# A fused convolution, linear attention and mixed feed-forward kernel: the state matmuls, the halves of z and the orders of the first phase

## The reference

```python
x = einsum('oc,bchw->bohw', inv(I - ricker_circulant(width, damp)), x)   # x: 16 x 128 x 32 x 32
t = tokens(x)                                    # 16 batches x 1024 tokens x 128
# linear attention, 8 heads of 16, on u = layernorm(t)
Q, K = elu(u @ W_q.T) + 1, elu(u @ W_k.T) + 1;  V = u @ W_v.T
S = cumsum(K outer V, over tokens);  z = cumsum(K, over tokens)
t = t + ((Q . S) / max(Q . z, 1e-6)) @ W_out.T
# feed-forward, whose weights are merged per batch by a gate, on u = layernorm(t)
g = mean over tokens(relu(u @ gfc1_w.T + gfc1_b) @ gfc2_w.T + gfc2_b)
W1m, b1m, W2m, b2m = base + g mixed with the 8 task vectors
t = t + layernorm(u + relu(u @ W1m.T + b1m) @ W2m.T + b2m) * lng + lnb
```

## Time and profile before

| | us |
|---|---|
| median of 3 runs | 847.6 (845.93 to 848.53) |
| the profiled execution | 848.7 |
| its span, first to last instruction | 846.9 |
| last start of `make_qk` (tile 128 of 128) | 547.6 |
| first instruction after the first phase's tiles on VectorE | 571.2 |

### The profile page before, as it was taken

How to read it: one execution, slowest core, us unless ns; L and a number is a source line. 1 busy time by engine, 2 the same in 40 slices (tenths; PEclk the granted TensorE clock), 3 DMA queues, 4 the chain that set the end, 5 groups by cost and what they waited for, 6 DMA issues and landing times. The chain is left out here.

```text
span 846.9 us, 37199 instructions
## 1 busy us (share of the span) xinstructions
PE 739.7 (87%) x11168; PEld 538.4 (64%) x11168; DVE 742.6 (88%) x2736; ACT 670.2 (79%) x1875; POOL 534.6 (63%) x1009
## 2 busy tenths in 40 slices
PE   1588999999999999999999999968899998899994
PEld 1255666666666666666666666648577777577773
DVE  6587999999999999999999999955788985689894
ACT  1477898999989989998898988844788885688884
POOL 5486888888888888888988988810133342033333
PEclk9888999999999999999999999977999999999998
DMA  2255444454444444544454444410022221122222
GB/s 80 52 126 118 98 111 105 92 117 109 91 111 106 105 105 100 116 106 99 106 111 95 116 100 98 88 33 26 2 77 86 77 74 51 38 64 76 74 87 75
DMA packets 165473, 74.10 MB, mean 87 GB/s; under 512 B 139212, under 2 KB 152687, under 8 KB 165368
## 3 DMA queue, kind: packets, MB, share of 16 engines
q1 hardware_dynamic: 165432, 73.58, 36.0%
HBM read 22.69 MB, written 17.30 MB: 47 GB/s over the span
## 5 line engine op out<-in xcount | busy, mean ns | idle before, releaser
L795 DVE SCALAR_TENSOR_TENSOR scores_lo<-p_a,scores_hi 128x512 f16<-128x512 f32 x256 | 164.0, 682 | 0.0
L698 ACT ACTIVATE scores_hi<-p_a 128x512 f16<-128x512 f32 x256 | 138.5, 600 | 6.4 <-PE p_a L543 6.2
L861 POOL TENSOR_TENSOR stats<-stats,consts 128x1 f32<-128x1 f32 x128 | 78.1, 610 | 75.7 <-DVE stats L745 75.6
L1312 POOL TENSOR_TENSOR ffn_rstd_shift<-ffn_rstd_shift,consts 128x4 f32<-128x4 f32 x32 | 36.7, 1146 | 132.8 <-DVE ffn_rstd_shift L1271 132.8
L886 POOL TENSOR_TENSOR qk_parts<-qk_f,qk_parts 128x128 f16<-128x128 f32 x256 | 104.9, 429 | 0.1
L867 POOL TENSOR_TENSOR stats<-stats,consts 128x1 f32<-128x1 f32 x128 | 89.0, 695 | 18.7 <-DVE stats L751 17.1
L560 PE MATMUL p_o<-v_parts,scores_hi 128*128 128x17 f16 x1024 | 90.2, 171 | 12.1 <-ACT scores_hi L698 6.2
L560 PEld LDWEIGHTS p_o<-v_parts,scores_hi 128*128 128x128 f16 x1024 | 80.4, 96 | 30.0 <-issue 27.6
L1095 PE MATMUL psb<-merged_W_of_batch,h_hi 128*128 128x128 f16 x512 | 94.2, 220 | 4.9 <-DVE h_lo L1249 3.8
L1249 DVE TENSOR_TENSOR h_lo<-h_f,h_hi 128x512 f16<-128x512 f32 x128 | 95.0, 782 | 1.2 <-ACT h_hi L1152 1.2
L1141 ACT ACTIVATE h_f<-psb,merged_b_of_batch 128x512 f32<-128x512 f32 x128 | 87.0, 711 | 11.4 <-PE psb L1076 11.3
(11 more groups left out here) (195 smaller groups left out, 3009.6 us busy)
## 6 DMA issues: line engine op xcount, KB each, us to landing
x_f<-in_x SPq DMA_DIRECT2D x32, 256.0 KB, 2.9
t_rows<-t SPq DMA_DIRECT2D x64, 128.0 KB, 1.9
t_back<-t_rows SPq DMA_DIRECT2D x32, 256.0 KB, 2.6
out<-out_tile SPq DMA_DIRECT2D x32, 256.0 KB, 2.0
tv_share<-in_L_ffn_tv_W SPq DMA_DIRECT2D x32, 128.0 KB, 2.2
qkT_parts<-qk_parts SPq DMA_TRANSPOSE x128, 3.1
base_ffn_weights<-in_L_ffn_W SPq DMA_DIRECT2D x2, 256.0 KB, 4.3
W_hi_lo_rows<-base_parts SPq DMA_DIRECT2D x4, 128.0 KB, 3.8
```

Of the source, the lines that this page charges most:

```text
L698: nc.scalar.activation(ah[:, t % 2, cols], p_a[:, cols], ACT.Relu).then_inc(ahi_ready[eo], 1)
L795: nc.vector.scalar_tensor_tensor(al[:, t % 2, cols], p_a[:, cols], 0.0, ah[:, t % 2, cols], ALU.max, ALU.subtract).then_inc(alo_ready[eo], 1)
```

## The change

Five things are done, all of them in the first phase; the code of the second is the same.

- **State.** `state` makes each head's block alone: 16 matmuls with 64 columns of weights and 17 or 16 columns of output, even heads into partitions 0 to 63 and odd ones into 64 to 127. The off-diagonal blocks are never written (the bank is cleared once), so the mask multiplication is gone. `state_hi` is a ScalarE copy out of PSUM, `state_lo` a VectorE subtraction out of PSUM; GpSimd has no part in it.
- **z.** `z_hi` (ScalarE) and `z_lo` (GpSimd) split z in SBUF, before it is turned, and SyncE turns both parts with one transposing DMA of 128x256 float16. TensorE's `turn_z` and VectorE's `z_lo` are gone. `gate` waits for that DMA.
- **High parts.** `q_hi` moves from ScalarE to GpSimd.
- **Banks.** `gate` moves from p_m1 to p_m2, beside `turn_out`.
- **Orders.** All five tables are new. The last skew grows from 8 to 11, so two batches are written out ahead of the loop and two behind it.

```diff
-TENSOR_ORDER = [("conv", 0), ("project", 0), ("turn_out", 5), ("gate", 8), ("values", 4), ("turn_z", 7),
-                ("state", 2), ("out_project", 5), ("scores", 2)]
+TENSOR_ORDER = [("scores", 3), ("conv", 0), ("gate", 11), ("state", 2), ("project", 0), ("out_project", 6),
+                ("values", 4), ("turn_out", 5)]
...
+GPSIMD_ORDER = [("split_x", 0), ("rsqrt2", 9), ("z_lo", 10), ("q_hi", 1), ("k_hi", 1), ("rsqrt1", 0), ("qk_lo", 1)]
+SYNC_ORDER = [("turn_z", 10), ("load_x", 3), ("load_tv", 3), ("store", 8), ("turn", 1)]
...
-        zh = sb(top, "zT_hi", [P, NT * P], F16)
-        zl = sb(top, "zT_lo", [P, NT * P], F16)
+        zz = sb(top, "zT_hi_lo", [P, 2, NT * P], F16)
+        zh, zl = zz[:, 0, :], zz[:, 1, :]
...
             def run(eng, order, stages):
                 stages = [(skew, stages[name]) for name, skew in order]
-                batch(stages, 0, old=False)
-                with eng.Fori(1, B) as b:
+                for b in range(2):
                     batch(stages, b)
-                batch(stages, B, new=False)
+                with eng.Fori(2, B) as b:
+                    batch(stages, b)
+                for b in range(B, B + 2):
+                    batch(stages, b)
...
+                    def turn_z(b, t):
+                        n = TILES * b + t
+                        parts = n + 1 if isinstance(n, int) else sp.to_reg(n + 1)
+                        sp.wait_ge(ones_set, 1)
+                        sp.wait_ge(zlo_ready, parts)
+                        sp.dma_start_transpose(zz[:, :, bass.ds(n * P, P)],
+                                               zp[:, t % 4, :, :].rearrange("p w c -> p (w c)"))\
+                            .then_inc(z_turned[t % 4], 16)
...
-                        at_least(pe, sm_ready, (TILES - 1) * b + t)
-                        for a in range(NP):
-                            kk = pk[:, t % 4, 1, 2 * a:2 * a + 2, :].rearrange("p h c -> p (h c)")
-                            mm(sbank[:, a, :], kk, vp[:, t, 2 * a:2 * a + 2, 0:VW],
-                               start=(t == 0 and a == 0), stop=False, skip_group_check=True)
-                            last = mm(sbank[:, a, :].rearrange("p (h w) -> p h w", w=VW)[:, :, 0:DH], kk,
-                                      vp[:, t, 2 * a:2 * a + 2, VW:VW + DH],
-                                      start=False, stop=True, skip_group_check=True)
+                        at_least(pe, sp_ready, (TILES - 1) * b + t)
+                        for h in range(NH):
+                            e, kk = h % 2, pk[:, t % 4, 1, h, :]
+                            o = sbank[64 * e:64 * e + 64, h // 2, e * VW:(e + 1) * VW]
+                            mm(o, kk, vp[:, t, h, 0:VW], start=(t == 0 and h < 2), stop=False, skip_group_check=True)
+                        for h in range(NH):
+                            e, kk = h % 2, pk[:, t % 4, 1, h, :]
+                            o = sbank[64 * e:64 * e + 64, h // 2, e * VW:e * VW + DH]
+                            last = mm(o, kk, vp[:, t, h, VW:VW + DH], start=False, stop=True, skip_group_check=True)
...
                     def gate(b, t):
                         n = TILES * b + t
-                        pe.wait_ge(zhi_ready, n + 1)
-                        pe.wait_ge(zlo_ready, n + 1)
+                        pe.wait_ge(z_turned[t % 4], 32 * b + 16 * (t // 4 + 1))
                         bank_read("gate", n)
-                        g = p_m1[:, P:2 * P]
+                        g = p_m2[:, P:2 * P]
...
+                    def state_hi(b, t):
+                        if t == TILES - 1:
+                            return
+                        m = (TILES - 1) * b + t
+                        act.wait_ge(su_done, m + 1)
+                        at_least(act, av_done, TILES * b + t - 2)
+                        nc.scalar.activation(sp2[:, t % 4, 0, :, :], sbank, ACT.Copy).then_inc(sh_ready, 1)
...
-                        nc.scalar.activation(zh[:, bass.ds(n * P, P)], p_m2[:, P:2 * P], ACT.Copy).then_inc(zhi_ready, 1)
+                        nc.scalar.activation(zp[:, t % 4, 0, :], z_[:, t % 2, :], ACT.Copy).then_inc(zhi_ready, 1)
...
-                        nc.vector.tensor_tensor(sm[:, t % 2, :, :], sbank,
-                                                kcol("blk").unsqueeze(1).broadcast_to([P, NP, 2 * VW]), ALU.mult)\
-                            .then_inc(sm_ready, 1)
+                        dve.wait_ge(sh_ready, m + 1)
+                        nc.vector.tensor_tensor(sp2[:, t % 4, 1, :, :], sbank, sp2[:, t % 4, 0, :, :], ALU.subtract)\
+                            .then_inc(sp_ready, 1)
...
-                        nc.vector.tensor_tensor(zl[:, cols], p_m2[:, P:2 * P], zh[:, cols], ALU.subtract)\
-                            .then_inc(zlo_ready, 1)
...
+                            dst = dst[:, :, :, 0, :] if w == 0 else dst[:, :, 0, :, :]
+                            nc.gpsimd.tensor_copy(dst, src.unsqueeze(2).broadcast_to([P, NH, 2, DH])).then_inc(done, 1)
...
+                        nc.gpsimd.tensor_tensor(zp[:, t % 4, 1, :], z_[:, t % 2, :], zp[:, t % 4, 0, :], ALU.subtract)\
+                            .then_inc(zlo_ready, 1)
```

More of the change, by code:

```diff
@@ L914, in _ @@
                     run(pool, GPSIMD_ORDER, {"rsqrt1": rsqrt1, "qk_lo": qk_lo,
[L915 to L916 removed]
+                        "split_x": split_x,
+                        "rsqrt2": rsqrt2, "q_hi": qk_hi(0, qhi_ready), "k_hi": qk_hi(1, khi_ready), "z_lo": z_lo})
         with ExitStack() as pb:
```

158 lines of the change are left out of this document (64 added, 94 removed).

## The result

| | before | after |
|---|---|---|
| median of the runs | 847.5 us | 877.65 us (872.9 to 881.5) |
| profiled execution, span | 846.9 us | 879.6 us |
| ratio, 95% interval | | 1.0355 [1.0293, 1.0417] |
| period, starts of `make_qk` 24 to 104 | 4.043 us | 4.220 us |
| last `make_qk` starts at | 547.6 us | 570.9 us |

The span grew by 32.7 us: 23.3 up to the last `make_qk`, 6.9 in the drain of the pipeline, 2.4 in the second phase. The forecast of 809 us is missed by 69 us, and its sign is wrong. A measured time is the median of a kernel's runs; for the last experiment that is the median of two runs at 955.0 and 956.5 us, since its two others, at 979.9 and 987.2 us, ran at a lower granted clock.

What follows compares the result with a forecast made beforehand. VectorE was taken as the bound, its period falling from 4.045 to 3.70 us, 41 us over some 120 tiles. 848.7 - 41 - 3 + 5 = 809.7 us profiled, 808.6 as median, stated as 809; range 789 to 850.

Steps and rivals of the forecast that it cites:

- What bounds the kernel now: First phase, steady tiles: VectorE, busy 97.9 of 100 us, sets the 4.045 us period; 3.57 without collisions after the change.
- It becomes lighter: ScalarE, 3.65 us per tile, loses q_hi, swaps a read, gains a 136-column copy: lighter by 0.1 to 0.2 us.
- the waits at the projection should go: TensorE's projection waits 0.31 us per slot for VectorE's v_lo; this goes, since v_lo comes in the slot before.
- Collisions, 0.13 us: VectorE's normalise and make_qk waiting for GpSimd after the change: 0.13 us per tile, bounds nothing to 0.66; VectorE's period 3.70.
- GpSimd, 3.46 us: Work per tile unchanged at 3.46 us: state_hi and state_lo go (0.79), q_hi and z_lo come (0.79); slack 0.24.
- TensorE, 3.46 us: Work per tile: 3.43, less 0.14 for turn_z, plus 7/8 x 0.19 for state's 16 matmuls; between 3.29 and 3.9.
- its rival: TensorE becomes the bound: 64-column weights load slower, state costs 0.9 us, TensorE needs 3.9; 838 us, chance 0.12.
- z's transfer: no stall: SyncE's second transposing DMA lands within nothing to 3.1 us; z has about 3 us until the gate, so no stall.
- Startup, -3 us: At the ninth tile the scores waited 4.9 us for turn; an extra slot hides most: 3 us gained (0 to 5).
- Drain, +5 us: Fill and drain of the first phase: three more short slots at 1 to 3 us each, 5 us (3 to 10).
- Second phase, nothing: The second phase's code is untouched, so its time changes by nothing.
- Slower: normalise and make_qk both collide in most slots, VectorE needs 4.23 us: 872 us; chance 0.15 including unforeseen costs.

Runs made afterwards that it cites:

- the last experiment: The version of 833.6 us with the gate moved behind values, ahead of turn_out alone, in TensorE's order: 955.7 us.
- the two cuts: Kernel after with one order entry moved: z_hi behind copy_out on ScalarE, 842.1 us; or gate behind project on TensorE, 841.6 us.
- the two copies: Kernel after plus one unread 128x128 ScalarE copy per slot: between z_hi and copy_out (on the ring) 904.7 us; ahead of read_t1 (off it) 876.8 us.
- The narrow `z_lo`: Kernel before with VectorE's z_lo over 2 of 128 columns, the rest of z's low part left at zero: 846.2 us.
- the z part alone: Kernel before with only the change's z part (z_lo on GpSimd, turning by transfer, gate at ten slots), other orders as before: 850.8 us.
- the version of 833.6 us: Kernel after with normalise moved behind eps1 on VectorE and z_hi behind copy_out on ScalarE: 833.6 us, 0.9839 of the kernel before.
- the state part alone: Kernel before with only the change's state part, state_hi first in ScalarE's order, z and other orders as before: 924.25 us.
- the wide state: Kernel after with state as 8 matmuls of 128 weight columns, as before the change, and no mask: 865.7 us.

## Why the prediction was wrong, step by step

**"What bounds the kernel now": the step that failed.** I took the fullest engine for the bound and let the period follow its sum (4.045 - 0.20 - 0.05 - 0.22 = 3.57). In the kernel after, no engine's sum sets the period: it is 4.22 us with VectorE busy for 89.3 of 100, and a ring of waits through the orders of three engines holds it, as the two cuts (36 us each) and the two copies (27 us on the ring, nothing off it) show. The narrow `z_lo` refutes the subtraction for the kernel before as well: 0.11 us less work on VectorE, the busy share unchanged, 0.05 us gained. In the z part alone the busy share fell by 7 and the period not at all, though there GpSimd was at 93. I had the mechanism in hand, having written that `make_qk` ends 0.28 us behind `x_lo`, but I did not draw from it that the wait is elastic. Nor did I ever walk from one slot to the same place in the next along the orders.

**"It becomes lighter", "the waits at the projection should go".** Both sentences count work on an engine whose order had changed, and name what goes. What came instead was `z_hi` ahead of `copy_out` on ScalarE and the gate ahead of `state` on TensorE, and with `scores_hi` behind `state_hi` and `normalise` behind `scores_lo` the ring. Each single cut gave 36 us. That is two thirds of what was missing to the forecast's period: 4.22 as it is, 3.88 to 3.90 with one arrow cut, 3.81 in the best order that I found, 3.70 forecast.

**Collisions, 0.13 us.** The mechanism was right, the places nearly so. `make_qk` came free (0.378 on average, I had 0.40 to 0.50 for it), and `normalise` collides: 0.12 us more on average. The size was met (I had 0.13 for both together), but it lies on the ring rather than in slack. Two readings were off. In the earlier trace rows I had a case of the rule that the first to issue keeps the ports; there `normalise` started first, by 0.04 us, and was still the one that waited. And `make_qk` does meet `z_lo`, in 83 of 95 slots, but there it is `z_lo` that waits.

**GpSimd, 3.46 us.** Mis-sized: `z_lo` I had as half of a pair, 0.40 us; the page of the kernel after gives 0.646 for it on average.

```profile
L893 POOL TENSOR_TENSOR z_parts<-z,z_parts 128x128 f16<-128x128 f32 x128 | 82.7, 646 | 69.5 <-ACT z_parts L708 44.7
...
x_f<-in_x SPq DMA_DIRECT2D x32, 256.0 KB, 3.1
...
zT_hi_lo<-z_parts SPq DMA_TRANSPOSE x128, 2.3
```

(Count, busy us and mean ns, idle time before; then the DMA issues with the time to landing.) The shortest takes 0.42, so my price was that of one left alone: GpSimd waits for VectorE as VectorE does for GpSimd. In the 83 slots where `z_lo` overlaps `make_qk` it ends 0.28 or 0.29 us behind it. In the version of 833.6 us its mean is 0.48. It didn't matter in the kernel after (84.4 of 100), and did more in the z part alone (93.3).

**TensorE, 3.46 us, and its rival.** Near in size, with a part that I had not counted. From the first of the 16 small matmuls (314.56) to the projection (314.92) are 0.36 us; I had 0.40, and 0.9 in the rival. The Trainium skill's page TensorEngine Tiling (Array Packing), on which that rival leaned, names the loss of the fast weight load with column tiling ("Restrictions"). By the starts in the trace (medians, 100 to 500 us) the small matmuls go in pairs, the two of a pair 0.003 to 0.009 us apart and the pairs 0.032, so each costs no more than a full one of the earlier trace rows. But `state` has a pause at either end that the full weights do not have. Behind the same `turn_z` (L595) it starts 0.237 us on in the state part alone (304.14 to 304.37) and 0.145 in the kernel before, and what follows its last matmul starts 0.109 us behind that, against 0.026 before and 0.047 with the wide state. The second pause is within the 0.36 us; the 0.09 us of the first were in no term of mine. That they are the change of the tiling is a reading: the number of matmuls changed as well. In the kernel after the first one does not show, since the 0.43 us ahead of `state` are as long with untiled weights.

**z's transfer: no stall.** Right in the steady part. It lands after 2.3 us (the row above); the waits of the gate's weights for it come in the drain: 13.6 us in 8 times from 560 to 604 us.

```profile
PEld p_m L606 <- DMA zT_hi_lo<-z_parts: 13.6, 8, 2.4
```

**Startup, -3 us.** Not there. The scores at the ninth tile waited for `turn` even longer than in the earlier trace rows, 5.5 us against 4.9.

**Drain, +5 us.** It was 6.9. From the last z to the gate's sums are 4.2 us before, 8.4 after and 7.1 with the z part alone; and the last z itself comes 2.7 us later behind the last `make_qk` than before. So some 3 to 4 us go with the transfer (between `z_lo` and the gate), and 2.7 with the later slots of `normalise`. With the z part alone the drain is still only 25.1 us, since z comes earlier there. What shortens it was not found.

**Second phase, nothing.** 2.4 us more (274.9 to 277.3), but in the profiled executions of the experiments, whose second phases are all the same code, it lies anywhere from 273.1 to 277.3. One execution each can't tell this from nothing.

**The rivals.** TensorE was not the bound, z was late in the drain alone, the orders did not fit. (By its own period of 3.9 us, the case of a late z is 832 or 833 us, not 831; nothing hangs on it.) "Slower" had the right sign and 872 us was near to 877.65, but for the wrong reason: it wanted both collisions in most slots and VectorE full. The last sentence of the prediction, on a chain of waits around the slot if no engine is full, is what came true, and it had no price and hardly a chance.

## What to carry to other kernels

Where orders are written out by hand, sums per engine are at best a lower bound and no forecast: start at one step, follow who lets it go (data, the buffer's last reader, the instruction ahead on the same engine) until you are at the same step one slot later, and add it up. Do so for each order that the change touches, above all where an engine waits for another in the middle of its slot. A busy share near 100% may hold waits that give way, and a swap of two entries can be worth more than the work removed: here 36 us against 14 us net of the whole change in its best order.

## What the runs showed of the hardware

- A VectorE instruction from SBUF to SBUF that meets GpSimd's work can last longer by 0.33 us (`normalise`, 0.347 to 0.676 us), also with 127 columns rather than 128. The Trainium skill tells of the shared ports on its page SBUF — State Buffer ("Who interferes with whom"). The traces agree that one of the two waits until the other is through: all 35 `normalise` of the kernel after (100 to 500 us) that start while `x_lo` runs end 0.08 us behind it. Which one waits, the starts do not tell when they are close. With the copy on the ring, 9 `normalise` start 0.06 to 0.09 us ahead of `x_lo` and still wait for it, 0.81 to 0.84 us long; one that starts 0.18 us ahead does not. In the kernel after, 60 `z_lo` start 0.05 to 0.07 us ahead of `make_qk` and wait for it.
- 16 matmuls with 64 weight columns, alternating between the halves of the array, start in pairs 0.032 us apart, where 8 with 128 columns start 0.025 us apart. Going into them costs some 0.09 us more (0.237 us behind the matmul ahead against 0.145) and coming out 0.06 to 0.08 (0.109 against 0.047 and 0.026).
- `state` starts some 0.43 us behind the gate, 0.35 of it idle by the profile as "issue", tiled or not. With the gate not held up the pause can be as short as 0.15 us, but is not always. The cause is open.
- A transposing transfer of a quarter of the size is hardly cheaper to issue (1.17 us on SyncE against 1.23) and lands after 2.3 us instead of 3.1.
